# A conditioned recurrence in 1024 steps: the next state's early part in two pieces, sum banks seeded by copies

## The reference

```python
ae = layernorm(cond) * g + b;  h = gelu(ae @ w1 + b1);  xa, xb = split(h @ w2 + b2)
layer = base[None] + einsum('bdr,bkr->bdk', xa, xb)
y = x + (x + einsum('btc,bco->bto', x, layer))      # y = 2 x + x @ layer
def step(prev_h, xw):                                # xw = y_t @ Wx + b
    next_h = tanh(prev_h @ Wh + xw);  return next_h, next_h
out = y + scan(step, cond, xW)
```

## Time and profile before

| | |
|---|---|
| median of the three runs | 792.67 us |
| the profiled execution | 791.64 us |
| its span | 789.8 us |
| PE busy | 736.8 us (93%) |
| PEld busy | 679.7 us (86%) |
| DVE busy | 258.3 us (33%) |
| ACT busy | 396.4 us (50%) |
| matmuls, activations | 21105, 3092 |

### The profile page before, as it was taken

How to read it: one execution, slowest core, us unless ns; L and a number is a source line. 1 busy time by engine, 2 the same in 40 slices (tenths; PEclk the granted TensorE clock), 3 DMA queues, 4 the chain that set the end, 5 groups by cost and what they waited for, 6 DMA issues and landing times.

```text
span 789.8 us, 48134 instructions
## 1 busy us (share of the span) xinstructions
PE 736.8 (93%) x21105; PEld 679.7 (86%) x21105; DVE 258.3 (33%) x1411; ACT 396.4 (50%) x3092; POOL 6.4 (1%) x18
## 2 busy tenths in 40 slices
PE   6699999999999999999999999999999999999996
PEld 5688888888888888888888888888888888888885
DVE  6433333333333333332333332323333333333322
ACT  6355545555555555555555554555555555554554
POOL 3000000000000000000000000000000000000000
DMA  7000000000000000000000000000000000000000
GB/s 271 7 10 9 11 11 9 7 11 9 10 11 9 7 11 9 10 10 10 7 10 10 10 10 10 10 8 10 10 10 10 10 7 9 11 10 9 8 7 6
DMA packets 12285, 12.51 MB, mean 16 GB/s; under 512 B 1813, under 2 KB 11056, under 8 KB 12080
## 3 DMA queue, kind: packets, MB, share of 16 engines
q1 hardware_dynamic: 11984, 9.45, 4.1%
q0 software_dynamic: 96, 0.02, 0.0%
HBM read 7.36 MB, written 2.10 MB: 12 GB/s over the span
## 4 chain that ended last, share of the span: by engine, by line
PE 88%; ACT 6%; issue 3%; DMA 1%; SPq 1%; DVE 1%; DVEq 0%; another core or an unknown queue 0%
PE acc L320 48%; PE pre L320 16%; PE p_y L278 8%; PE acc L297 7%; ACT h_pre L456 6%; PE pre L297 4%; PE p_xo L273 2%; PE p_xo L268 1%; DMA x_in<-x_dram 1%; PE acc L294 1%; PE pre L294 1%; SPq L212 1%; PE p_y L413 0%; SPq L209 0%; DVE lay_s L684 0%
## 5 line engine op out<-in xcount | busy, mean ns | idle before, releaser
L320 PE MATMUL acc<-h_pre,wh_s 128*128 128x2 f16 x8192 | 504.8, 168 | 35.7
L320 PEld LDWEIGHTS acc<-h_pre,wh_s 128*128 128x128 f16 x8192 | 378.5, 106 | 90.6 <-ACT h_pre L456 73.5
L456 ACT ACTIVATE h_pre<-pre 128x4 f16<-128x4 f32 x1023 | 178.0, 174 | 377.8 <-PE pre L320 377.8
L563 DVE TENSOR_TENSOR h_lo<-h_f,h_pre 128x4 f16<-128x4 f32 x1024 | 166.8, 163 | 512.6 <-ACT h_f L462 511.5
L320 PE MATMUL pre<-h_rnd,wh_s 128*128 128x2 f16 x4092 | 263.4, 168 | 0.0
L320 PE MATMUL acc<-h_lo,wh_s 128*128 128x2 f16 x4096 | 250.9, 165 | 0.0
L320 PEld LDWEIGHTS pre<-h_rnd,wh_s 128*128 128x128 f16 x4092 | 190.6, 108 | 0.0
L320 PEld LDWEIGHTS acc<-h_lo,wh_s 128*128 128x128 f16 x4096 | 188.4, 104 | 0.0
L462 ACT ACTIVATE h_f<-acc 128x4 f32<-128x4 f32 x1024 | 177.9, 174 | 0.6 <-PE acc L320 0.6
L464 ACT ACTIVATE h_rnd<-acc 128x4 f16<-128x4 f32 x1022 | 173.2, 169 | 0.0
L297 PE MATMUL acc<-y_s,wx_s 128*128 128x16 f16 x2048 | 101.8, 175 | 0.0
(11 more groups left out here) (77 smaller groups left out, 161.1 us busy)
## 6 DMA issues: line engine op xcount, KB each, us to landing
w_f<-w_dram SPq DMA_DIRECT2D x8, 512.0 KB, 7.6
x_in<-x_dram SPq DMA_DIRECT2D x32, 64.0 KB, 2.3
out_dram<-o_row SPq DMA_DIRECT2D x64, 32.0 KB, 1.9
w_f<-w_dram SPq DMA_DIRECT2D x1, 256.0 KB, 2.7
base_f<-base_dram SPq DMA_DIRECT2D x1, 256.0 KB, 10.2
wh_f<-wh_dram SPq DMA_DIRECT2D x1, 256.0 KB, 9.8
wx_f<-wx_dram SPq DMA_DIRECT2D x1, 256.0 KB, 9.9
cond_r<-cond_dram SPq DMA_DIRECT2D x1, 2.0 KB
```

The lines of the kernel that those rows point to most:

```text
L320: return nc.tensor.matmul(dst[:, mo, :], wh_s[:, pw, ki, mo * P:(mo + 1) * P], h[:, par, ki, :], start=False, stop=True, skip_group_check= ...
L456: nc.scalar.activation(h_pre[:, n % 2].rearrange("p m b -> p (m b)"), src, func, scale=scale).then_inc(s_hpre[(n // HALF) % 2], 1)
L563: nc.vector.tensor_sub(h_lo[:, par].rearrange("p m b -> p (m b)"), h_f[:, slot, :], h_pre[:, par].rearrange("p m b -> p (m b)")).then_inc( ...
```

## The change

- The early part comes in two pieces. `pre[half]` becomes two banks, one for each output tile mo. The four products of h_rnd go tile by tile, and each pair raises `s_presum`; ACT writes `h_pre` in two activations of 128x2, each with its own wait; PE waits for the pieces one after the other, and all eight products of h_pre stand ahead of the h_rnd products.
- The sum banks are seeded by DVE. The input products are computed only into `pre`, 18 a half, six behind each of u = 2, 3 and 4. `acc` is two banks instead of four, used by both halves (`z_cols`). At u = 9 and 10 DVE waits until ACT has read the bank, and copies the other half's input part out of `pre` into the bank of even steps, then into that of odd steps (`seed`, 128x32 each); PE takes `s_seed` ahead of u = 10 and 11.
- ACT writes the f32 tanh for DVE into a tile of its own in SBUF, `p_f`; the copy in `h_f` for the output is a fourth kind of activation (after h_pre, p_f and h_rnd), issued last. With h_pre in two pieces ACT runs five activations a step. `sum_out` waits for the new `s_hkeep`.
- `x_s` and the layer's output bank hold their steps next to each other. Turned x, layer sums and turned output share one bank, `p_w`. All 32 layer products go behind A's u = 8 to 12, seven to a step (four in the last). `turn_x` moves to A's u = 5, DVE's work on x to u = 6 and 7, on y to u = 13 to 15.
- Two of PE's three clears move behind u = 6, the third behind u = 7.

The diff, cut; the removed bodies of `half_a` and `half_b` are left out.

```diff
...
-        x_s = sb("x_s", [P, 2, BLOCK, NM, NB], F16)
+        x_s = sb("x_s", [P, 2, NM, NB, BLOCK], F16)
...
-        acc = [[pb(f"acc{half}{par}", [P, 512]) for par in range(2)] for half in range(2)]
-        pre = [pb(f"pre{half}", [P, 512]) for half in range(2)]
-        p_xo = pb("p_xo", [P, 512])
-        p_y = pb("p_y", [P, 512])
+        acc = [pb(f"acc{par}", [P, 512]) for par in range(2)]
+        pre = [pb(f"pre{half}", [P, NM, 512]) for half in range(2)]
+        p_w = pb("p_w", [P, 512])
+        p_f = sb("p_f", [P, COLS])
...
-        PRE = 2
-        INPUT = [(slot, *product) for slot in (0, PRE, 1) for product in PRODUCTS]
-        BEFORE = 2 * len(PRODUCTS)
+        INPUT = sorted(PRODUCTS, key=lambda product: product[0])
 
         TILES = [(mo, ki) for mo in range(NM) for ki in range(NM)]
+
+        FILL, LAYERS, SEED = 2, 8, 10
+
+        def z_cols(half, u):
+            at = (half * (HALF // 2) + u // 2) * COLS
+            return slice(at, at + COLS)
...
             def layer_products(todo):
-                py = p_y[:, 0:P].rearrange("p (t m b) -> p t m b", m=NM, b=NB)
+                py = p_w[:, P:2 * P].rearrange("p (m b t) -> p m b t", m=NM, b=NB)
                 for bb, mo, ki, pw, px in todo:
-                    last = nc.tensor.matmul(py[:, :, mo, bb], lay_s[:, pw, bb, ki, mo * P:(mo + 1) * P],
-                                            x_s[:, px, :, ki, bb], start=(bb, mo, ki, pw, px) == LAYER[0],
+                    last = nc.tensor.matmul(py[:, mo, bb, :], lay_s[:, pw, bb, ki, mo * P:(mo + 1) * P],
+                                            x_s[:, px, ki, bb, :], start=(bb, mo, ki, pw, px) == LAYER[0],
                                             stop=True, skip_group_check=True)
                 return last
...
             def input_products(half, todo):
 
 
-                for slot, mo, ki, pw, py in todo:
-                    if slot == PRE:
-                        dst, n, t = pre[half], HALF, slice(half * HALF, (half + 1) * HALF)
-                    else:
-                        dst, n, t = acc[half][slot], PAIRS, slice(half * HALF + slot, half * HALF + slot + HALF - 1, 2)
-                    dst = dst[:, 0:n * COLS].rearrange("p (t m b) -> p t m b", m=NM, b=NB)[:, :, mo, :]
+                t = slice(half * HALF, (half + 1) * HALF)
+                for mo, ki, pw, py in todo:
+                    dst = pre[half][:, mo, 0:HALF * NB]
                     out_channels = slice(mo * P, (mo + 1) * P)
                     if ki is None:
-                        nc.tensor.matmul(dst, b_w[:, out_channels], ones[:, 0:n * NB], start=mo == 0, stop=True,
-                                         skip_group_check=True)
+                        last = nc.tensor.matmul(dst, b_w[:, out_channels], ones[:, :], start=True, stop=True,
+                                                skip_group_check=True)
                     else:
-                        nc.tensor.matmul(dst, wx_s[:, pw, ki, out_channels], y_s[:, py, t, ki, :],
-                                         start=False, stop=True, skip_group_check=True)
+                        last = nc.tensor.matmul(dst, wx_s[:, pw, ki, out_channels], y_s[:, py, t, ki, :],
+                                                start=False, stop=True, skip_group_check=True)
+                return last
...
             def clear_states(half):
 
                 pe.sem_clear(s_hpre[half])
                 pe.sem_clear(s_hrnd[half])
-                pe.sem_clear(s_hlo[half])
 
             def chain_step(half, u, last=False):
 
 
                 par = u % 2
-                full = acc[half][par][:, (u // 2) * COLS:(u // 2 + 1) * COLS].rearrange("p (m b) -> p m b", b=NB)
-                early = pre[half][:, u * COLS:(u + 1) * COLS].rearrange("p (m b) -> p m b", b=NB)
+                full = acc[par][:, z_cols(half, u)].rearrange("p (m b) -> p m b", b=NB)
 
                 def onto(dst, pw, mo, ki, h):
-                    return nc.tensor.matmul(dst[:, mo, :], wh_s[:, pw, ki, mo * P:(mo + 1) * P], h[:, par, ki, :],
+                    return nc.tensor.matmul(dst, wh_s[:, pw, ki, mo * P:(mo + 1) * P], h[:, par, ki, :],
                                             start=False, stop=True, skip_group_check=True)
 
-                pe.wait_ge(s_hpre[half], u + 1)
-                for mo, ki in TILES:
-                    onto(full, 1, mo, ki, h_pre)
-                for mo, ki in TILES[:3]:
-                    onto(full, 0, mo, ki, h_pre)
+                for ki in range(NM):
+
+                    pe.wait_ge(s_hpre[half], NM * u + ki + 1)
+                    for mo in range(NM):
+                        for pw in range(2):
+                            onto(full[:, mo, :], pw, mo, ki, h_pre)
                 if not last:
                     pe.wait_ge(s_hrnd[half], u + 1)
-                    for mo, ki in TILES:
-                        done = onto(early, 0, mo, ki, h_rnd)
-                    done.then_inc(s_presum[half], 1)
-                for mo, ki in TILES[3:]:
-                    onto(full, 0, mo, ki, h_pre)
+                    for mo in range(NM):
+                        for ki in range(NM):
+                            done = onto(pre[half][:, mo, u * NB:(u + 1) * NB], 0, mo, ki, h_rnd)
+                        done.then_inc(s_presum[half], 1)
                 pe.wait_ge(s_hlo[half], u + 1)
                 for mo, ki in TILES:
-                    done = onto(full, 0, mo, ki, h_lo)
+                    done = onto(full[:, mo, :], 0, mo, ki, h_lo)
                 done.then_inc(s_sum[half], 1)
 
...
+            def half_steps(half, first=False, last=False):
 
 
                 for u in range(HALF):
-                    chain_step(A, u)
-                    if first and u == 0:
-                        input_products(A, INPUT[BEFORE:])
-                    if not first and u == 1:
+                    if u >= SEED and u < SEED + 2 and not (last and half == B):
+
+                        take(pe, s_seed[u % 2], 1)
+                    chain_step(half, u, last=last and half == B and u == HALF - 1)
+                    if u == 1 and not first:
                         turn_out()
...
+                    if FILL <= u < FILL + 3 and not (last and half == B):
+                        if u == FILL and half == B:
+                            take(pe, s_ysplit, 1)
+                        filled = input_products(1 - half, share(INPUT, 6, u - FILL))
+                        if u == FILL + 2:
+                            filled.then_inc(s_fill, 1)
+                    if u == 6 and not first:
+                        clear_states(1 - half)
+                    if u == 7 and not first:
+                        pe.sem_clear(s_hlo[1 - half])
+                    if half == A and not last:
+                        if u == 5:
+                            turn_x()
+                        if u == LAYERS:
+                            take(pe, s_xsplit, 1)
+                        if LAYERS <= u < LAYERS + 5:
+                            product = layer_products(share(LAYER, 7, u - LAYERS))
+                        if u == LAYERS + 4:
+                            product.then_inc(s_ymm, 1)
...
-            input_products(A, INPUT[:BEFORE])
-            half_a(first=True)
+            input_products(A, INPUT).then_inc(s_fill, 1)
+            for par in range(2):
+                take(pe, s_seed[par], 1)
+            half_steps(A, first=True)
...
-            def give_pre(n, src, func, scale):
-
-                nc.scalar.activation(h_pre[:, n % 2].rearrange("p m b -> p (m b)"), src, func,
-                                     scale=scale).then_inc(s_hpre[(n // HALF) % 2], 1)
-
-            def give_h(n, src, func, scale, rounded=True):
+            def give_pre(n, m, src, func, scale):
+
+                nc.scalar.activation(h_pre[:, n % 2, m, :], src, func, scale=scale).then_inc(s_hpre[(n // HALF) % 2], 1)
+
+            def give_h(n, src, func, scale, rounded=True, final=False):
 
                 half = (n // HALF) % 2
-                nc.scalar.activation(h_f[:, (n - 1) % BLOCK, :], src, func, scale=scale).then_inc(s_hf[half], 1)
+                if not final:
+                    nc.scalar.activation(p_f[:, 0:COLS], src, func, scale=scale).then_inc(s_hf[half], 1)
                 if rounded:
                     nc.scalar.activation(h_rnd[:, n % 2].rearrange("p m b -> p (m b)"), src, func,
                                          scale=scale).then_inc(s_hrnd[half], 1)
+                nc.scalar.activation(h_f[:, (n - 1) % BLOCK, :], src, func, scale=scale).then_inc(s_hkeep[half], 1)
...
                     if not final:
-                        act.wait_ge(s_presum[half], u + 1)
-                        give_pre(n, pre[half][:, u * COLS:(u + 1) * COLS], ACT.Tanh, 1.0 / SCALE)
+                        for m in range(NM):
+                            act.wait_ge(s_presum[half], NM * u + m + 1)
```

(54 more changed lines are left out.)

114 lines of the change are left out of this document (35 added, 79 removed).

## The result

Six runs of the changed kernel gave 795.4 to 797.22 us, a median of 796.19 us; six of the kernel before, 791.72 to 793.39, a median of 792.95 us. The ratio is 1.0044, with a 95% interval from 1.0031 to 1.0057. The forecast was 782.2 us, 778.4 to 789.8. It was wrong in sign.

The account below looks back on a forecast made before the run. The prediction took the latency of three nearly equal loops, not PE's busy time, as the bound: 791.64 - 5.6 (h_lo loop) - 4.7 (clears) - 0.2 (ahead of the steps) = 781.1, plus 1.0 for the median: 782.2 us, range 778.4 to 789.8.

Parts of the forecast that it names:

- The h_lo loop, 5.6 us: Sum to DVE to PE's h_lo products to next sum: step falls from 0.7333 to 0.7278, 5.6 us over 1023 steps.
- the step stays at 0.733: Rival: the h_lo loop has nothing to give and only the clears count; 787.8 us, 12%.
- The clears, 4.7 us: PE's three semaphore clears behind turn_out, moved behind u = 6 and 7: all 63 long steps go, 4.7 us.
- The guess's loop at 0.71 and room beside the h_lo loop: Loops of the guess (h_pre) and h_rnd each fall from 0.74 to 0.71, leaving only the h_lo loop.
- The 2% rival, that steps would fall to 0.71: The h_lo loop has more to give and steps match the two other loops' 0.71; 768 us, 2%.
- Activations: On ACT, five a step need 0.35 to 0.40 of 0.73 us, the fourth kind in idle time; cost 0.
- The rival of waiting activations 0.13 apart: ACT becomes the bound: waiting activations can't start closer than 0.13, f32 tanh 0.08 late each step; 864 us, 4%.
- Seeds: Two DVE PSUM-to-PSUM copies of 128x32 a half, 0.19 us taken, 0.16 to 0.29 as ends; cost 0.
- Layer products: On PE, contiguous on both sides, pitch falls from 0.053 to 0.027; seven take 0.19 and fit a step's free time.
- Ahead of the steps, 0.2 us less: Before the first step: shorter layer products and input products against product landing, two seeds and three clears; net 0.2 us less.
- Input products, 2304 fewer: worth nothing: 36 of 54 a half go, 62 us of PE's queue, all in idle time; worth nothing.

Follow-up runs that it names:

- e3_strided: The kernel before with x_s alone laid out by step as in the change, the layer's output in PSUM left four elements apart; 800.3 us, 1.0109 of before.
- e1_write: The changed kernel with DVE's two split operations on x writing front to back and picking steps out of PSUM; 785.07 us, 0.9921 of the kernel before.
- f10_again: e1_write timed and profiled once more, unchanged; 781.84 us.
- e2_clears: The kernel before with only PE's three clears moved away from the turned output, as in the change; 786.79 us against 791.87.
- e6_lo3_after: e1_write without the fourth h_lo product in each step; 754.82 us, 0.9524 of the kernel before.
- f9_nopf: e1_write with four activations a step instead of five, DVE reading the f32 tanh from h_f in SBUF; 782.01 us.
- e8_psum: e1_write with p_f, the f32 tanh for DVE, in the eighth PSUM bank instead of SBUF; 768.51 us, 0.97 of the kernel before.

## Why the prediction was wrong, point by point

The forecast missed the median by 14.0 us. Two terms, of 9.1 and 5.2 us, make up nearly all of it.

- **DVE's work on x, written in the new layout.** This is the step that failed. The prediction wrote for the new layout only what PE gains from it. For the two DVE operations that write it the sum has no term: they were put at nothing, without a length and without a cover. They write 2-byte elements 64 bytes apart and take 0.71 us; the cover was what is left of a step on DVE, and h_lo stands in the same queue behind them. That costs 9.1 us in the steps, 0.4 of it from the later x of the first block (e3_strided alone: 8.4 us). Ahead of the steps they cost 0.2 to 0.3: from DVE's copy of x_f to its first h_lo it is 11.17 us, against 10.94 in e1_write and 10.89 in f10_again. The Trainium skill's "Vector Engine (DVE) Microarchitecture Reference", section 5.2, Measured stream behaviour on trn2, lets a port stream at full rate only in runs of two or more adjacent 4-byte words, and gives 1.7 to 2.5 ns an element where the destination hops or steps with every element, against 1.05. The runs agree in direction and go beyond it in size, for 2-byte elements: (0.71 - 0.28) / 128 is 3.4 ns more for each. I had looked up the PSUM side of a pattern that changes on both sides.
- **The h_lo loop, 5.6 us.** The other term that failed: the changed kernel got 0.4 of it. The mechanism was read rightly. In the plain steps of the kernel before, PE's first load for h_lo follows the load ahead of it by 0.027, so PE's queue set the step; in the changed kernel the distance is 0.050, so PE waits for h_lo. The loads came 0.003 to 0.005 earlier, as forecast (+0.427 before, +0.423 in the changed kernel, +0.421 in e1_write, in ns starts). But in the steps of 0.733 the four products run 0.108 from the first load to the last start, where they ran 0.105 before; with 0.727 they run 0.104. So the term came in nearly whole in e1_write's and f10_again's profiled executions, and in none of the six runs of the changed kernel. That a step takes only some lengths, and that this floor lies between two of them, no row rounded to 0.01 could show. The rival "the step stays at 0.733", with 12%, was right for the changed kernel.
- **The clears, 4.7 us.** Right: 4.8 by the traces of both kernels and 5.1 in e2_clears.
- **The guess's loop at 0.71 and room beside the h_lo loop.** Right in kind: removing an h_lo product shows in full (e6_lo3_after, whose 0.700 a step says that the two other loops need no more than that), and it doesn't in the old order. The 2% rival, that steps would fall to 0.71, fell.
- **Activations.** Right: f9_nopf. The rival of waiting activations 0.13 apart is refuted by the pairs at L447, which start 0.068 to 0.069 apart in ns starts.
- **Seeds.** Right: 0.199 for 0.19, and no step at u = 10 or 11 is longer.
- **Layer products.** Right: a mean of 188 ns, one each 0.027, and no step with seven of them is longer. e3_strided shows that the output side did it.
- **Ahead of the steps, 0.2 us less.** Not decided: the first guess came 0.9 later, and one kernel's own executions differ by as much.
- **Input products, 2304 fewer: worth nothing.** Right: no step with or without them differs, before and after.

With the one omission mended the time lies in the forecast's range: 782.2 us said, 785.07 and 781.84 us measured for e1_write. How near it comes to 782.2 depends on which length its steps take.

## What to carry to other kernels

When a layout changes so that a reader gets contiguous data, cost the writer too, operation by operation, and then ask what latency stands behind it in its queue; often only the order of the writer's walk has to be turned. In a recurrence, compare full and empty steps first: if they are equally long, count loops and not busy time, and shorten all that close at nearly the same length, since a gain in one shows only when the others have room. Then look at where each operand of the last loop lies.

## What the runs showed of the hardware

- DVE writing 128 f16 elements a partition 64 bytes apart: 0.71 us, against 0.28 contiguous (e1_write, e3_strided). Reading f32 from PSUM 16 bytes apart costs nothing (0.28 in e1_write), nor does reading it 128 bytes apart (the y_new group, 288 ns in either kernel).
- Matmul output of 32 f32 columns 16 bytes apart in PSUM: one each 0.053 us (e3_strided, and the earlier trace rows); in runs of two, or contiguous (the changed kernel), 0.027.
- An activation of 128x4 f32 to PSUM instead of SBUF takes 158 ns instead of 173 and lets DVE start 15 ns sooner, and DVE reads it there in the same 0.16 us (e8_psum). The Trainium skill, "ScalarE: Activation LUTs", Step-by-step: what each stage is for, calls PSUM the lower-latency destination of an activation; the runs agree, and no loss on DVE's side came with it.
- A semaphore clear on PE costs its queue 0.11 to 0.12 us: in ns starts the three in the window of the earlier trace rows begin at 397.551, 397.672 and 397.789, and the next load at 397.897. Three in a row behind a transpose cost a step 0.07.
- The loop across PE, ACT and DVE took a whole number of 6.67 ns in every step of thirteen traces, and one kernel (f9_nopf) ran once in 786 us, with most steps at 0.7333, and four times in 781 to 783.
